# Delta-rule recurrence: the state is updated once in 32 steps instead of once in 16, with one more cross product inside

## What is computed

```
def step(S, inp):
    qt, kt, vt, at, bt = inp
    err = einsum('bhij,bhj->bhi', S, kt) - vt
    S = at[..., None] * S - bt[..., None, None] * (err[..., None] * kt[:, :, None, :])
    o = einsum('bhij,bhj->bhi', S, qt)
    return (S, o)
```

## Time and profile before

| | |
|---|---|
| median of three executions | 3903.03 us |
| profiled execution | 3909.59 us |
| its span | 3907.8 us |
| recurrence, first to last P transpose | 151.3 to 2310.5 us |
| TensorE busy / VectorE busy / GpSimd busy | 82% / 76% / 56% of the span |
| mean granted TensorE clock | 0.92 |

### The profile page before, as it was taken

One profiled execution on the slowest core, in us unless ns is written; L12 is line 12 of the kernel. 1 busy time (PEld: TensorE's weight loads), 2 busy tenths in 40 slices (PEclk: granted clock), 3 DMA queues, 4 the chain that ended last, 5 costly groups with the idle time before them and its releaser, 6 DMA issues. The chain is left out here.

```text
span 3907.8 us, 126216 instructions
## 1 busy us (share of the span) xinstructions
PE 3194.9 (82%) x53441; PEld 2377.5 (61%) x53441; DVE 2965.5 (76%) x6600; ACT 2040.0 (52%) x4394; POOL 2182.6 (56%) x2735
## 2 busy tenths in 40 slices
PE   3678888887888888788888854759999899898989
PEld 2556666665666666666666644636666567656765
DVE  4488888888888888888888882058888788847884
ACT  2334444444444444444444423338887699728982
POOL 1367776767767677776767663431101188508860
PEclk7889999999999999999999975879999999999999
DMA  2111111111101111110111104100000012101111
GB/s 74 31 40 41 29 50 33 44 40 39 43 29 49 34 42 41 36 47 27 45 32 40 37 27 135 44 22 2 2 2 2 20 29 45 32 19 28 40 37 27
DMA packets 155957, 140.03 MB, mean 36 GB/s; under 512 B 64976, under 2 KB 108236, under 8 KB 155138
## 3 DMA queue, kind: packets, MB, share of 16 engines
q1 hardware_dynamic: 153090, 129.25, 12.0%
q0 software_dynamic: 2304, 2.71, 0.2%
HBM read 96.12 MB, written 16.82 MB: 29 GB/s over the span
## 5 line engine op out<-in xcount | busy, mean ns | idle before, releaser
L1235 DVE TENSOR_TENSOR a_tmp<-a_h,banks 128x128 f32<-128x128 f32 (+6 forms) x896 | 436.0, 487 | 29.9 <-DVE a_h L1212 0.2
L1241 DVE TENSOR_REDUCE a_h<-a_tmp 128x64 f32<-128x128 f32 (+6 forms) x896 | 432.2, 482 | 8.8
L940 POOL TENSOR_TENSOR a_st<-a_st,a_ab 128x512 f32<-128x512 f32 x256 | 322.1, 1280 | 0.0
L694 PE MATMUL banks<-a_wt,a_kt 32*64 32x64 f32 x8192 | 163.1, 258 | 145.8 <-DVE a_wt L1278 141.1
L552 PE MATMUL banks<-a_xseg,a_w_q 128*128 128x128 f32 x2048 | 247.0, 277 | 38.9 <-ACT a_kq L766 36.1
L2105 ACT ACTIVATE c_s<-c_s,c_low 128x384 f32<-128x384 f32 (+1 forms) x512 | 266.3, 579 | 19.1 <-DVE c_low L2049 13.7
L694 PEld LDWEIGHTS banks<-a_wt,a_kt 32*64 32x64 f32 x8192 | 153.6, 166 | 198.2 <-DVE a_wt L1278 169.8
L552 PEld LDWEIGHTS banks<-a_xseg,a_w_q 128*128 128x128 f32 x2048 | 234.3, 191 | 48.3 <-ACT a_kq L766 41.7
L2049 DVE CUSTOM_DVE_ANT_0 c_s<-banks,c_band 128x384 f32<-128x384 f32 (+1 forms) x512 | 245.5, 517 | 23.6 <-PE banks L1974 23.6
L552 PE MATMUL banks<-a_xseg,a_w_k 128*128 128x128 f32 x2048 | 241.5, 277 | 21.4 <-DMA a_xseg<-xn 18.4
L2150 POOL TENSOR_TENSOR c_qm<-c_qT,c_heads 128x512 f32<-128x512 f32 x32 | 33.3, 1040 | 396.3 <-PE banks L1974 395.9
(11 more groups left out here) (318 smaller groups left out, 8888.8 us busy)
## 6 DMA issues: line engine op xcount, KB each, us to landing
a_ab<-decays SPq DMA_DIRECT2D x512, 128.0 KB, 3.0
d_Vs<-d_V SPq DMA_DIRECT2D x128, 128.0 KB, 2.3
sent<-k_nothing SPq DMA_DIRECT2D x40, 64.5 KB, 2.3
b_xe<-sent SPq DMA_DIRECT2D x8, 322.5 KB, 3.4
a_xseg<-xn SPq DMA_DIRECT2D x32, 70.0 KB, 2.5
a_xrow<-in_L_attn_x SPq DMA_DIRECT2D x128, 16.0 KB, 1.8
x<-a_xrow SPq DMA_DIRECT2D x128, 16.0 KB, 1.6
back<-k_nothing SPq DMA_DIRECT2D x32, 64.0 KB, 1.6
```

The lines of the kernel that those rows point to most:

```text
L694: t = e.matmul(self.ubank(bi)[par * DK:(par + 1) * DK, ct * DK:(ct + 1) * DK], self.Kt[rows, k0:k0 + DK], self.Wt[rows, x:x + 2, :].rearra ...
L940: e.tensor_tensor(sv, sv, self.ab[:, 8 * n:8 * n + 8, :], ALU.mult).then_inc(*self.s_decay.at((g, n)))
L1235: e.tensor_tensor(prod, both, gram, ALU.mult).then_inc(*step.at((g, t, "product")))
L1241: e.tensor_reduce(self.results(ch, t), prod, AX.X, ALU.add).then_inc(*step.at((g, t, "w")))
```

## The change

A segment is now one chunk of 32 steps in four quarters of 8 (`QK`, `NQ`). P for all 32 steps is taken from the state at the start of the segment, in two products after each other, with a buffer for each. The cross product occurs three times (after quarters 0, 1 and 2); the middle one carries the updates of the first 16 steps into all of the last 16, for which ScalarE keeps one more copy of the Gram products (`Gh`) and GpSimd corrects P of the second half (`pool_half`, `pool_from_half`). The state update, its decay and the spreading of the decays occur once a segment. The order on each engine is rewritten. The scale and the turn of a segment move one segment later. In the diff, `-` and `+` lines of the parts that matter:

```
@@ -462,19 +464,20 @@
...
-            self.P2, self.tmp = sb("p2", [P, 32, CK, 2]), sb("tmp", [P, 2, 32, CK])
+            self.P2, self.tmp = two("p2_", [P, 32, CK, 2]), sb("tmp", [P, 2, 32, QK])
...
     def pe_P(self, e, q, s, ch):
-        g, kq, pb = 2 * s + ch, self.kq[s % 2], self.c.bank(4, 2)
+        kq, pb = self.kq[s % 2], self.c.bank(4, 2)
         js = slice(ch * CK, (ch + 1) * CK)
-        if g:
-            q.wait_ge(self.s_p2, g - 1)
+        if ch:
+            q.wait_ge(self.s_p2, (s, 0))
+        elif s == 0:
+            q.wait_ge(self.s_zeroed, 1)
         else:
-            q.wait_ge(self.s_zeroed, 1)
-        if g >= 3:
-            q.wait_ge(self.s_moment, ("mean", s - 1) if ch else ("dev", s - 2))
-        if ch == 0 and s >= 3:
-            q.wait_ge(self.s_evac, ("out", s - 3))
+            q.wait_ge(self.s_p2, (s - 1, 1))
+            if s >= 2:
+                q.wait_ge(self.s_moment, ("dev", s - 2))
+            if s >= 3:
+                q.wait_ge(self.s_evac, ("out", s - 3))
         for pair in range(0, NB, 2):
-            if g:
-                q.wait_ge(self.s_st if pair else self.s_state, (g - 1, pair + 1))
+            if s and ch == 0:
+                q.wait_ge(self.s_st if pair else self.s_state, (s - 1, pair + 1))
...
         for s in range(self.nseg):
-            old, older, nxt, g = s - 1, s - 2, s + 1, 2 * s
+            old, older, nxt = s - 1, s - 2, s + 1
             more = nxt < self.nseg
             self.pe_P(e, q, s, 0)
+            self.pe_P(e, q, s, 1)
+            if more:
+                for half in range(2):
+                    self.pe_project_rows(e, q, "a", nxt, half)
+                for half in range(2):
+                    self.pe_project(e, q, "k", nxt, half)
+            self.pe_cross(e, q, s, 0)
             for n in range(2):
                 self.pe_time_rows(e, q, s, n)
             if old >= 0:
                 self.pe_moment(e, q, old, "mean")
-            for n in range(2):
-                if older >= 0:
+            if more:
+                for half in range(2):
+                    self.pe_project(e, q, "q", nxt, half)
+            self.pe_cross(e, q, s, 1)
+            if more:
+                for n in range(2):
+                    self.pe_gram(e, q, nxt, n)
+            if older >= 0:
+                for n in range(2):
                     self.pe_turn(e, q, older, n)
-            for n in range(2):
-                if older >= 0:
+                for n in range(2):
                     self.pe_gate(e, q, older, n)
             if more:
-                for half in range(2):
-                    self.pe_project_rows(e, q, "a", nxt, half)
-            self.pe_cross(e, q, s, 0)
+                self.pe_project_rows(e, q, "v", nxt, 0)
+            self.pe_cross(e, q, s, 2)
             if more:
-                for half in range(2):
-                    self.pe_project(e, q, "k", nxt, half)
-                self.pe_project(e, q, "q", nxt, 0)
-            self.pe_carry(e, q, g)
-            self.pe_U(e, q, s, 0)
-            g += 1
-            self.pe_P(e, q, s, 1)
-            if more:
-                self.pe_project(e, q, "q", nxt, 1)
-                for n in range(2):
-                    self.pe_gram(e, q, nxt, n)
+                self.pe_project_rows(e, q, "v", nxt, 1)
+            if older >= 0:
+                self.pe_out(e, q, older)
             if old >= 0:
                 self.pe_moment(e, q, old, "dev")
-            if older >= 0:
-                self.pe_out(e, q, older)
-            self.pe_cross(e, q, s, 1)
-            if more:
-                for half in range(2):
-                    self.pe_project_rows(e, q, "v", nxt, half)
-            self.pe_carry(e, q, g)
-            self.pe_U(e, q, s, 1)
+            self.pe_carry(e, q, s)
+            self.pe_U(e, q, s)
...
+        e.activation(self.Gh[:, :, :, heads].rearrange("p z t r -> p r z t"), v[:, 1], ACT.Identity, scale=rows_of[:, 2:3],
+                     bias=rows_of[:, 3:4]).then_inc(*self.s_gh.at((s, par)))
...
         for s in range(self.nseg):
-            old, older, nxt, g = s - 1, s - 2, s + 1, 2 * s
+            old, older, nxt = s - 1, s - 2, s + 1
             more = nxt < self.nseg
+            if old >= 1:
+                self.act_root(e, q, old - 1)
+            if more:
+                for half in range(2):
+                    self.act_project_rows(e, q, "a", nxt, half)
+                for half in range(2):
+                    self.act_project(e, q, "k", nxt, half)
+            self.act_cross_gram(e, q, s, 2)
             for n in range(2):
                 self.act_time_rows(e, q, s, n)
+            if more:
+                for half in range(2):
+                    self.act_project(e, q, "q", nxt, half)
+            self.act_gram_bank(e, q, 2 * s + 1)
+            self.act_gate_rows(e, q, 2 * s + 1)
+            if more:
+                for n in range(2):
+                    self.act_gram(e, q, nxt, n)
             if older >= 0:
                 for n in range(2):
                     self.act_affine(e, q, older, n)
                 for n in range(2):
                     self.act_gate(e, q, older, n)
             if more:
-                for half in range(2):
-                    self.act_project_rows(e, q, "a", nxt, half)
+                self.act_project_rows(e, q, "v", nxt, 0)
             if old >= 0:
                 self.act_square(e, q, old)
             if more:
-                for half in range(2):
-                    self.act_project(e, q, "k", nxt, half)
-                self.act_project(e, q, "q", nxt, 0)
-            self.act_state(e, q, g)
-            self.act_gram_bank(e, q, g + 1)
-            self.act_gate_rows(e, q, g + 1)
-            if more:
-                self.act_project(e, q, "q", nxt, 1)
-                for n in range(2):
-                    self.act_gram(e, q, nxt, n)
+                self.act_cross_gram(e, q, nxt, 0)
+                self.act_project_rows(e, q, "v", nxt, 1)
             if older >= 0:
                 self.act_out(e, q, older)
-            if old >= 0:
-                self.act_root(e, q, old)
+            self.act_state(e, q, s)
             if more:
-                self.act_cross_gram(e, q, nxt)
-                for half in range(2):
-                    self.act_project_rows(e, q, "v", nxt, half)
-            self.act_state(e, q, g + 1)
-            if more:
-                self.act_gram_bank(e, q, g + 2)
-                self.act_gate_rows(e, q, g + 2)
+                self.act_gram_bank(e, q, 2 * s + 2)
+                self.act_gate_rows(e, q, 2 * s + 2)
...
+    def pool_half(self, e, q, s):
+        both = self.P2[1][:].rearrange("p i t z -> p i (t z)")
+        q.wait_ge(self.s_p2, (s, 1))
+        q.wait_ge(self.s_cum, (s, "last"))
+        over = self.last[s % 2][:, 0, :].rearrange("p (i o) -> p i o", o=1).broadcast_to([P, 32, SEG])
+        e.tensor_tensor(both, both, over, ALU.mult).then_inc(*self.s_rest.at((s, "half")))
+        q.wait_ge(self.s_rest, (s, "half"))
+        self.pool_less(e, q, s, 2)
+    def pool_from_half(self, e, q, s):
+        P2, X = self.P2[1], self.X
+        q.wait_ge(self.s_xt, (s, 1))
+        e.tensor_tensor(P2[:, :, 0:QK, 1], P2[:, :, 0:QK, 1], X[:, :, CK:CK + QK], ALU.subtract).then_inc(*self.s_rest.at((s, "half", "q")))
+        later = P2[:, :, QK:, :]
+        e.tensor_tensor(later, later, X[:].rearrange("p i (z t) -> p i t z", z=2)[:, :, QK:, :],
+                        ALU.subtract).then_inc(*self.s_rest.at((s, "half", "later")))
...
         for s in range(self.nseg):
-            old, older, nxt, g = s - 1, s - 2, s + 1, 2 * s
+            old, older, nxt = s - 1, s - 2, s + 1
             more = nxt < self.nseg
-            self.pool_rest(e, q, s, 0)
-            self.pool_history(e, q, s, 0, HAND, HC)
-            self.pool_second_half(e, q, s, 0)
+            self.pool_rest(e, q, s)
+            for t in range(HAND, QK):
+                self.pool_history(e, q, s, t)
+            self.pool_next(e, q, s, 0)
             for n in range(2):
-                self.pool_decay(e, q, g, n)
-            self.pool_cross(e, q, s, 0)
-            self.pool_first_half(e, q, s, 0)
-            for n in range(2):
-                if old >= 0:
-                    self.pool_centre(e, q, old, n)
-            for n in range(2, 4):
-                self.pool_decay(e, q, g, n)
+                self.pool_decay(e, q, s, n)
+            self.pool_cross(e, q, s, 1)
+            self.pool_older(e, q, s, 0)
             self.pool_query(e, q, s, 0)
             self.pool_prepare(e, q, s, 1)
+            self.pool_half(e, q, s)
+            if older >= 0:
+                self.pool_scale(e, q, older)
+            for n in range(2, 4):
+                self.pool_decay(e, q, s, n)
+            if more:
+                self.pool_cumulate(e, q, nxt, 0, 2)
+            self.pool_cross(e, q, s, 2)
+            for t in range(2 * QK + HAND, 3 * QK):
```

(94 more changed lines are left out.)

487 lines of the change are left out of this document (253 added, 234 removed).

## The result

The kernel after takes 4110.19 us (median of 4 runs, 4100.05 to 4110.52), the kernel before in the same session 3902.68 us (4 runs). The ratio is 1.0526, with a 95% interval of 1.0508 to 1.0544: 5% slower. The profiled execution took 4110.15 us, with a span of 4108.4 us and a mean granted clock of 0.877 (before 0.92).

A forecast was written before the change was run, and what follows sets the result against it. VectorE bounds the kernel, so gain must come from its idle time. New waits make a segment 74.5 us against 67.5: 3909.6 + 203 − 14 = 4098.6, 4092 as median, said as 4090 us; range 3970 to 4150.

The forecast's parts named there:

- (b): Rival: TensorE's clock stays down through v and the third cross, +5 us; segment 77.8, 4188 us; chance 0.12.
- (a): Rival: TensorE's clock holds at v; segment 72.75, 4041 us, or 4027 if P is warm too; chance 0.25.
- (c): Rival: third cross isn't late, only GpSimd's tail and late P stay; 67.65 a segment, 3893 us; chance 0.08.
- (d): Rival: nothing is late, VectorE sets the time; 62.9 us a segment, 3756 us; chance 0.07.
- P to X0: From a segment's first P transpose to its first cross transpose on VectorE: 15.75 us, where VectorE alone needs 14.0.
- W1 to X2: From the second Wt transpose to the third cross transpose on VectorE: 23.4 us of chain plus 1.75 for the clock.
- ST to P: From the state adds to the next segment's P transpose: 6.05 us with P cold, 4.8 at full clock.
- First place: Third cross waits behind ScalarE's Gram copies, affines, table load, gate and half of v: 23.4 us against VectorE's 18.2.
- The clock at v: TensorE's clock falls in the second pause before v, so v starts 0.5 and ends 1.8 us later; charged 1.75.
- Second and third place: GpSimd's tail puts the state adds 16.7 us after the third cross transpose; P waits for the deviation moment, 6.05 us.
- First cross: TensorE's second P, a, k and cross put the first cross transpose at 15.75 us after P; input load just in time.
- The ends, and the base: First two segments, last segment and work behind the loop, −8 to −14 us, taken as −14; base segment 67.5 us.

The follow-up runs named there:

- third cross first: Kernel after, with the third cross ahead of the two gates and both halves of v in TensorE's order: 4001.94 us, ratio 1.0242 to before.
- fewer copies: Kernel after with input slices loaded early, and three of four small Gram copies per half left out on ScalarE: 3966.88 us, ratio 1.0162 to before.
- the two edits: Each alone on the kernel after: GpSimd's query part ahead of the cumulated decays, 4150.82 us; deviation moment read before the output subtract, 4106.77 us.
- the first four experiments: On the kernel after: third cross moved ahead (1.0242), deviation moment read early (1.0514), query part early (1.0622), all three together (1.0414); ratios to before.
- kept warm: Kernel after with input slices loaded early, plus 16 identity products on TensorE after each U: 4008.78 us, ratio 1.0269 to before.
- five moves: Kernel after with third cross ahead, moment early, query early, slices loaded early, and v's first half in the Gram-copy wait: 3820.52 us, ratio 0.9768.

## Why the prediction was right

It said 4090 us, and the median is 4110.19. The three places are all there, and the segment of 75.2 us lies between the forecast's 74.5 and (b)'s 77.8, nearest to the forecast. Rival (a)'s condition came half true, v ran at full rate, and its time of 4041 did not. (c) and (d) are out, the third cross is late. The mechanism is right in its three places. That the number is so near is in part luck: two pairs of errors cancel, which are named below. By the forecast's own terms:

| term | predicted | after (median) |
|---|---|---|
| P to X0 | 15.75 | 16.79 |
| X0 to W1 | 10.85 | 10.95 |
| W1 to X2 | 25.15 | 24.80 |
| X2 to ST | 16.70 | 16.67 |
| ST to P | 6.05 | 5.92 |
| segment | 74.5 | 75.21 |

**First place, the chain of ScalarE.** Right in kind, shown by "third cross first" and "fewer copies". Its rows, against the earlier trace rows:

```profile
1223.89 0.80 ACT L799 ACTIVATE a_gh<-banks,k_cross_rows 128x256 f32<-128x256 f32 x1 [2.74 <-PE banks L584]
1224.49 0.64 ACT L801 ACTIVATE a_g<-banks 128x256 f32<-128x256 f32 x1
1225.16 2.40 ACT L805 ACTIVATE a_g<-banks 16x256 f32<-16x256 f32 x4
...
1231.28 2.91 ACT L882 ACTIVATE a_oT<-banks,a_lnb,a_lnw 128x128 f32<-128x128 f32 x8
1234.21 1.28 ACT L891 ACT_TABLE_LOAD   x1
1235.50 0.60 ACT L891 ACTIVATE a_og<-banks 128x512 f32<-128x512 f32 x1
```

The copies take 7.39 us (1231.28 − 1223.89) for my 7.75. The table load is 1.28 us and the gate starts right behind it. The Trainium skill ("ScalarE: Activation LUTs", section "What ACT_TABLE_LOAD costs") would add a drain; the measurement decides against it here.

**The clock at v.** Charged with 1.75 us for the wrong reason. TensorE's granted clock in windows of after, where the earlier trace rows has one of before (columns as in the earlier trace rows):

```profile
1223.00:1235.00 12.00, 5.98 (x124) 5.02 (x125) 11.35 (x22) 10.90 (x21) 7.42 (x12) 0.62 0.01 3
1236.30:1243.50 7.20, 7.20 (x178) 3.42 (x180) 1.37 (x2) 3.00 (x3) 0.97 (x2) 1.00 0.01 2
```

It falls in the pauses, as I chose, but it is back before v starts: v takes 3.64 us, its full rate (up to 4.21 in other segments). The slow part falls on the gates (3.62 instead of 2.05), where ScalarE's table load hides most of it. In its place came 1.02 us of "issue" in the middle of a Gram half, which the sum didn't have. ScalarE's first copy starts 6.52 us after W1 (1217.37 to 1223.89) where the sum had 2.1 + 2.0 + 1.15 = 5.25. Charge and omission nearly cancel, and that 25.15 meets 24.80 is luck.

**Second and third place.** GpSimd's tail came within 0.03 us, and P is late for the moment as worked out. Both are shown by the two edits, which took 1.74 and 2.60 us from their gaps.

**First cross.** This is the mis-sized term, 15.75 for 16.79. The first P of a segment and a were taken as they run in the chunk of before; now the second P runs wholly at the low clock in 8 of the 13 segments from 1000 to 2000 us (3.25 us, not half of it; 1.89 in the other five), a partly (2.37 instead of 1.8), and the load is not "just in time" in 7 of them. In this segment it is waited for 0.20 us, in others up to 3.2. The prediction did say that a warm P would find the load late. It didn't ask the same of every other gain, and this is what the first four experiments ran into. "A warm P gains little" is wrong once the load is early: kept warm, it gained 70 us.

**The ends, and the base.** From the first P of all to the first P of the last segment the time grew from 2124.25 to 2320.79 us, by 196.5; the sum had 203 − 6 = 197. Two errors cancel: the new segment is 0.8 us longer than summed (mean 75.34), and the old one's mean is 68.5, not the undisturbed 67.5 I took off. Behind the last segment's first P the time grew by 3.9 us, where I had taken 8 off. That sum, −8 + 5.6, was worked out and then not used; had I taken its −2.4, it would have given 4104 for the profiled execution, against 4110.15.

**What it had said would show.** The gap before the third X (6.73, predicted 5 to 7), the one before P (3.36, predicted 3 to 4, at a low clock) and VectorE's unchanged work are there; 1.79 stands before the output for "about 3"; before the first X it is 3.00 and not 1.7.

## What to carry to other kernels

Covering a wait with one engine's work helps only if the engine that ends the wait has its own instructions in the order of need: here five moves in the programs of TensorE, ScalarE, VectorE, GpSimd and SP turned +5.3% into −2.3%, without a change of the work. Cost each chain to its end with the rows of before, then ask of each gain what comes next; the input load, a few us behind, took away all that two right edits won. Nor is a gain kept by itself: what a filler of pauses is worth hangs on the pause it fills (2.5 us a segment won in one of 4.47 us, 1.3 lost in one of 0.5), so measure it again after each edit that closes one. And check an "issue" pause against the end of the operand's producer before you call it one of the engine.

## What the runs showed of the hardware

- TensorE makes short pauses inside blocks of products of one line, with nothing to wait for that the trace shows. From 1000 to 2000 us the kernel before has 35 of over 0.2 us (0.25 to 2.33 us, 26.6 in total), the kernel after 12 (0.30 to 1.21 us, 10.5 in total). Their places follow a count: from one to the next the trace of after has 1275, 892, 255, 3825, 1147, 2550, 1275, 892, 255, 1275 and 1275 matmul records, each within 0.5 of a multiple of 127.5; in before, all lie within 1.5 of one. That points to the position in the instruction stream and not to a semaphore. No run tested the cause. Not every multiple of 127.5 shows a pause. I had not costed them.
- The clock comes back under light or cold work by itself: after two pauses of 3.02 and 2.58 us the gates ran at half rate and v behind them at full rate. v placed directly in the pause ran at 0.56 instead (6.43 us for the 3.64 of full rate).
- The low clock has a price that can be bought back: 16 products of the identity in a 4.47 us pause were worth 2.5 us a segment, with the first P at 1.89 us instead of 3.25, and minus 1.3 us where the pause was 0.5 us.
